# Dividing 648 product columns at 384 instead of 512, and loosening the wait in front of the first routing product

## The chip, the cores and the metric

The kernel runs on one core of one Trainium2 chip. The metric is the device time of one execution in microseconds (us); lower is better. Everything is float32. TensorE multiplies in a rounded format (fp32r), so each operand is kept as a high part and a low part (the value minus its high part), and each product is three matmuls: high by high, high by low, low by high. The high part is made on ScalarE (ACT in the profile), the low part on VectorE (DVE).

## The reference

4096 tokens of width 512 pass through two blocks. Block 0 (a linear layer with per-batch low-rank additions, then a gated feed-forward) has nothing that the change touches. Block 1, in short:

```python
def cond(x, language_ids, W, Wr, A, B):
    base = jnp.einsum('btd,od->bto', x, W)
    logits = x @ Wr.T + 5.0 * one_hot(language_ids)
    gates = top-2 softmax of logits
    h = jnp.einsum('btd,erd->bter', x, A)
    return base + 2.0 * jnp.einsum('bter,bte,eor->bto', h, gates, B)

def ffn(y, W_base, b_base, W_router, A, B):
    gates = top-2 of softmax(y @ W_router.T), renormalised
    h = jnp.einsum('nd,erd->ner', y, A)
    return y @ W_base.T + b_base + 2.0 * (h * gates) @ B

x = x + ffn(cond(x))
```

Both are linear in their input but for the gates, so the kernel multiplies the weights once and runs the tokens through the folded weights.

## The kernel before

Tokens come in eight units of 512, the width in KC = 4 chunks of P = 128, so D = 512. E = 8 experts, and LH = E + 8*16 = 136 is the number of router and low-rank columns of one layer. All engines run their own instruction streams and meet by semaphores. Eight PSUM banks of 128x512 float32 exist: four accumulators (`acc`) and four that are handed out in turn (`ring`).

Block 0 takes about the first 794 us. Then comes **the fold**, `weight_product(i)` for i = 0 to 4: chunk i of the first layer's weights and low-rank factors (128 rows, `m2_hi`/`m2_lo`, the stationary operand) times the second layer's 648 columns (`rhs2_hi`/`rhs2_lo`, the moving operand): the 512 columns of its base weight and the 136 of its router and low-rank factors. Each is a sum over four parts of three matmuls, 12 matmuls to a bank, 24 to a chunk. The 512 columns go to a ring bank called "wide", the 136 to one called "slim".

When "slim" is complete, VectorE adds the identity to the 128 columns i*P of "wide" for i < 4 (the residual path; L1242). ScalarE copies "wide" to `m2_hi` (L921) over the operand just used, then "slim" to `xt_hi` (L924), for i = 4 to `ra2`. VectorE makes the low parts, `m2_lo` (L1244) and `xt_lo` (L1248). These last two free the banks: a ring bank is taken again four uses later, so "wide" of chunk i waits for that of chunk i - 2.

After the fold, TensorE runs `route_x(0)` and `route_x(1)`: for each of 4 token blocks of a unit, 12 matmuls with 272 moving columns, the 136 of the first layer (loaded) and the 136 folded ones. The first of them waits for the low parts of the tokens, for GpSimd's part of `xt_lo`, and for two counts:

```python
e.wait_ge(*ring_freed("wide", KC, 0))
e.wait_ge(*ring_freed("slim", KC - 1, 0))
```

ScalarE splits unit 1 (`split_unit(1)`, L936) between the fold and the copies of the routing banks (L943), VectorE does its half of that (L1229), then the router (`router(0, 0)`, from L1262) whose gated result (L1310) TensorE turns (`turn_h`, L1599). Then `out_base`, `route_h` and `out_close` form the output unit by unit; `out_base` is the first reader of the folded `m2_hi`/`m2_lo`. The helper `mm` at L1438 issues all matmuls but the transposes, so they are told apart by operand names and shapes.

SyncE's queue loads the units: `load_unit(1)` and `load_unit(2)` (L572) are issued when block 0's last matmul is done.

Of the kernel before, what the change touches and what calls it, by code (L numbers as in the profile page):

```python
# [6 lines left out]
ALU = mybir.AluOpType  # L7
ACT = mybir.ActivationFunctionType
AXX = mybir.AxisListType.X

P = 128
# [13 lines left out]
def plain(ap):  # L25
    return ap.bitcast(F32)


def build(nc, x, slots, langs, w0, b0, ab_table, w_gate, w_up, w_down, wb1, rhs2, ra1, b2t, b1, out):
    NT, KC, _, _ = x.shape  # L30
    D = KC * P
# [10 lines left out]
    LH = E + E * R  # L42
# [35 lines left out]
    def work(name, shape, dt):  # L78
        n = W
        for s in shape:  # L80
            n *= s
        h = sb(name, shape, dt, o[0])
        o[0] += (n + 31) // 32 * 32
        assert o[0] <= o[1], name
        return h
# [75 lines left out]
    m2_hi = work("m2_hi", [KC + 1, D], F32R)  # L161
    m2_lo_at = o[0]
    m2_lo = work("m2_lo", [KC + 1, D], F32R)
# [3 lines left out]
    xt_hi = work("xt_hi", [KC, 2 * LH], F32R)  # L167
    xt_lo = work("xt_lo", [KC, 2 * LH], F32R)
    ra2 = work("ra2", [LH], F32)
# [62 lines left out]
    sem = nc.alloc_semaphore  # L232
# [30 lines left out]
    pe_acc, pe_ring = sem("pe_acc"), sem("pe_ring")  # L263
# [16 lines left out]
    c_closed, l_closed = sem("c_closed"), sem("l_closed")  # L280
    act_freed, dve_freed = sem("act_freed"), sem("dve_freed")
    fold_hi_done, fold_lo_done = sem("fold_hi_done"), sem("fold_lo_done")
    m2_eye_done, m2_hi_done, xt_hi_done = sem("m2_eye_done"), sem("m2_hi_done"), sem("xt_hi_done")
    rows_done = sem("rows_done")
    dve_chain = sem("dve_chain")
    diff_done, expo_done, picked_done = sem("diff_done"), sem("expo_done"), sem("picked_done")
# [5 lines left out]
    def nth(t, m=KC - 1):  # L292
        return t * KC + m + 1
# [8 lines left out]
            c_ring += [("h", t + 1, 0, "dve")]  # L302
    l_ring = []
    for i in range(KC + 1):
        l_ring += [("wide", i, 0, "dve"), ("slim", i, 0, "dve" if i < KC else "act")]
    l_ring += [("rx", 0, c, "act") for c in range(TC)] + [("rx", 1, c, "act") for c in range(TC)]
    l_ring += [("th", 0, 0, "dve"), ("rh", 0, 0, "dve"), ("rh", 0, 1, "dve"), ("th", 0, 1, "dve")]
    l_ring += [("th", 1, 0, "dve"), ("rh", 1, 0, "dve"), ("rh", 1, 1, "dve")]
# [17 lines left out]
    def ring_bank(*use):  # L326
        return ring[ring_bank_at[ring_at[use]]]

    def ring_full(*use):
        return ring_at[use] + 1  # L330

    def ring_freed(*use):
        return freed_at[ring_at[use]]
# [76 lines left out]
    def l_slot(t):  # L410
        return t % 3
# [3 lines left out]
    def g_views(n):  # L415
        j, i = divmod(n, 7)
        i = ORDER[i]
        r = j % 2
        src = {1: wg_raw[r][:, 0:2, :], 2: wg_raw[r][:, 2:4, :], 4: wu_raw[r][:, 2:4, :],
               5: gs[r][0], 6: gs[r][1], 7: gs[r][2], 3: gs[r][3]}[i]  # L420
        hi, lo = (wring[n % N_W][:, half:half + 2 * P].rearrange("p (q c) -> p q c", q=2) for half in (0, 2 * P))
        return hi, lo, src[:, :, :]
# [9 lines left out]
        return dt_[n % 4][:, 0:c, 0, :], dt_[n % 4][:, 0:c, 1, :], src  # L432

    S_OF = {5: 1, 6: 2, 7: 3, 3: 4}


    fold_parts = [("wb1", i) for i in range(KC + 1)] + [("rhs2", k) for k in range(KC)]
# [314 lines left out]
    def act_program(e):  # L752
# [36 lines left out]
        def gate_up_hi(n):  # L789
            j, i = divmod(n, 7)  # L790
            i = ORDER[i]
            hi, _, src = g_views(n)
            if i in S_OF:
                e.wait_ge(gs_done, 4 * j + {7: 1, 5: 2, 6: 3, 3: 4}[i])
# [7 lines left out]
        def down_hi(n):  # L802
# [3 lines left out]
            else:  # L806
                g, i = d_steps[n]
                if i in S_OF:
                    e.wait_ge(ds_done, 4 * g + S_OF[i])
                else:  # L810
# [104 lines left out]
            e.activation(hi, first, ACT.Copy).then_inc(fold_hi_done, 1)  # L915

        def weight_product(i):
            e.wait_ge(pe_ring, ring_full("slim", i, 0))
            if i < KC:
                e.wait_ge(m2_eye_done, i + 1)  # L920
            e.activation(m2_hi[:, i, :], ring_bank("wide", i, 0)[:, :], ACT.Copy).then_inc(m2_hi_done, 1)  # L921
            bank = ring_bank("slim", i, 0)
            if i < KC:
                e.activation(xt_hi[:, i, LH:2 * LH], bank[:, 0:LH], ACT.Copy).then_inc(xt_hi_done, 1)  # L924
            else:
                e.activation(ra2[:, :], bank[:, 0:LH], ACT.Copy).then_inc(act_freed, 1)

        def split_unit(t):
            s = l_slot(t)
# [112 lines left out]
        for i in range(KC + 1):  # L1042
            weight_product(i)
# [35 lines left out]
    def dve_program(e):  # L1079
# [157 lines left out]
        def weight_product(i):  # L1237
            if i < KC:

                e.wait_ge(pe_ring, ring_full("slim", i, 0))  # L1240
                own = ring_bank("wide", i, 0)[:, i * P:(i + 1) * P]
                e.tensor_tensor(own, own, ident[:, :], ALU.add).then_inc(m2_eye_done, 1)  # L1242
            e.wait_ge(m2_hi_done, i + 1)
            e.tensor_tensor(m2_lo[:, i, :], ring_bank("wide", i, 0)[:, :], plain(m2_hi[:, i, :]),  # L1244
                            ALU.subtract).then_inc(dve_freed, 1)
            if i < KC:
                e.wait_ge(xt_hi_done, i + 1)
                e.tensor_tensor(xt_lo[:, i, LH:2 * LH], ring_bank("slim", i, 0)[:, 0:LH],  # L1248
                                plain(xt_hi[:, i, LH:2 * LH]), ALU.subtract).then_inc(dve_freed, 1)

        def over(ap):
            return ap[:, :].unsqueeze(2).to_broadcast([P, TC, E])
# [153 lines left out]
        for i in range(KC + 1):  # L1406
            weight_product(i)
# [28 lines left out]
    def pe_program(e):  # L1436
        def mm(out_ap, lhs, rhs, start, stop):
            return e.matmul(out_ap, lhs, rhs, start=start, stop=stop, skip_group_check=True)  # L1438

        def mm3(out_ap, w_hi, w_lo, v_hi, v_lo, start, stop):  # L1440
            mm(out_ap, w_hi, v_hi, start, False)
            mm(out_ap, w_hi, v_lo, False, False)
            return mm(out_ap, w_lo, v_hi, False, stop)

        def take_ring(*use):
            n = ring_at[use]
            first = len(c_ring)
            if n in range(first, first + 4):
                last_of_f = (out11_done, out21_done, out22_done, out12_done)[n - first]
                e.wait_ge(last_of_f, 2 * NS)  # L1450
            elif n >= 4:
                e.wait_ge(*freed_at[n - 4])
            return ring_bank(*use)
# [114 lines left out]
        def weight_product(i):  # L1568
            if i == 0:
                e.wait_ge(fold_lo_done, len(fold_parts))  # L1570
            wide, slim = take_ring("wide", i, 0), take_ring("slim", i, 0)
            for out_ap, cols in ((wide[:, :], slice(0, D)), (slim[:, 0:LH], slice(D, D + LH))):
                for k in range(KC):
                    part = slice(k * P, (k + 1) * P)
                    done = mm3(out_ap, m2_hi[:, i, part], m2_lo[:, i, part],
                               rhs2_hi[:, k, cols], rhs2_lo[:, k, cols], k == 0, k == KC - 1)
                done.then_inc(pe_ring, 1)

        def route_x(t):
            v = l_slot(t)  # L1580
            e.wait_ge(l_lo, nth(t))
            if t == 0:
                e.wait_ge(pool_late, 1)
                e.wait_ge(*ring_freed("wide", KC, 0))
                e.wait_ge(*ring_freed("slim", KC - 1, 0))
            for c in range(TC):
                bank = take_ring("rx", t, c)
                tok = slice(c * P, (c + 1) * P)
                for k in range(KC):
                    done = mm3(bank[:, 0:2 * LH], act_hi[v][:, k, tok], act_lo[v][:, k, tok],  # L1590
                               xt_hi[:, k, :], xt_lo[:, k, :], k == 0, k == KC - 1)
                done.then_inc(pe_ring, 1)
# [9 lines left out]
        def route_h(t):  # L1602
            e.wait_ge(hg1t_done, t + 1)
            if t == 0:
                e.wait_ge(*ring_freed("slim", KC, 0))
            for half in range(2):
                bank = take_ring("rh", t, half)
                for c2 in range(2):
                    c = 2 * half + c2
                    done = mm(bank[:, c2 * LH:(c2 + 1) * LH], hg1t[:, c * P:(c + 1) * P], ra2[:, :], True, True)  # L1610
                done.then_inc(pe_ring, 1)

        def out_base(t, m):
            v = l_slot(t)
            if t == 0:
                e.wait_ge((out11_done, out21_done, out22_done, out12_done)[m], 2 * NS)
            else:
                e.wait_ge(l_closed, nth(t - 1, m))
            if m == 0:
                e.wait_ge(l_lo, nth(t))  # L1620
            cols = slice(m * P, (m + 1) * P)
            for k in range(KC):
                mm3(acc[m][:, :], m2_hi[:, k, cols], m2_lo[:, k, cols],
                    act_hi[v][:, k, :], act_lo[v][:, k, :], k == 0, False)
            if m == 0:
                e.wait_ge(*ring_freed("th", 0, t))
            mm3(acc[m][:, :], m2_hi[:, KC, cols], m2_lo[:, KC, cols],
                hg1_hi[t % 2][:, :], hg1_lo[t % 2][:, :], False, False)
# [44 lines left out]
        for i in range(KC + 1):  # L1673
            weight_product(i)
        route_x(0)
        route_x(1)
        turn_h(0, 0)
        e.wait_ge(pool_late, 2)
# [8 lines left out]
        for m in range(KC):  # L1687
            out_close(0, m)
        route_x(2)
        turn_h(1, 1)  # L1690
        for t in range(1, NT):
# [97 lines left out]
```

## Time and profile before

| | us |
|---|---|
| median of 3 runs | 1025.44 |
| lowest, highest | 1023.64, 1025.75 |
| the profiled execution | 1019.78 |
| its span, first to last instruction | 1018.0 |
| TensorE busy in it | 1001.0 |
| VectorE busy | 550.1 |
| ScalarE busy | 437.9 |
| GpSimd busy | 188.5 |

Times in the rows are from the start of the span, which is 1.78 us shorter than the profiled execution. Matmuls are pipelined and their ends are modelled: the pace of TensorE is read from one start to the next, not from the duration of one matmul.

### The profile page before, as it was taken

The numbers are of one execution on the slowest core, as the hardware profiler recorded it, in microseconds if no ns is written. First come the engines' busy times: TensorE is split into PE (matmuls) and PEld (weight loads), VectorE is DVE, ScalarE is ACT, GpSimd is POOL, SyncE is SP. The second block draws the span as 40 slices with busy tenths as digits, with TensorE's granted clock in tenths as the row PEclk, the third lists the DMA queues.
The fourth block names the chain that finished last, engine by engine and source line by source line (L and its number), as shares of the span: only waits on it lengthen the run. The fifth ranks groups of instructions, "written<-read, shape, count | busy, mean of one in ns | idle before, by whom it ended". The sixth has DMA issues, their size and how long they took to land.

```text
span 1018.0 us, 13873 instructions
## 1 busy us (share of the span) xinstructions
PE 1001.0 (98%) x4835; PEld 841.2 (83%) x4835; DVE 550.1 (54%) x960; ACT 437.9 (43%) x821; POOL 188.5 (19%) x172
## 2 busy tenths in 40 slices
PE   8899998999999999999999999999999999999998
PEld 6888886888888888887888888888878888888886
DVE  3655466877785233586323497233296365555551
ACT  3655456555661333572333373333355133333321
POOL 3332022563400131400113220111350000000000
PEclk9999999999999999999999999999999999999999
DMA  9698667766977776877776777866796302222211
GB/s 320 226 344 296 241 208 274 264 238 235 291 272 232 215 194 194 274 227 258 235 196 193 241 229 253 278 192 196 193 354 222 131 1 84 93 86 91 84 42 62
DMA packets 111404, 210.18 MB, mean 206 GB/s; under 512 B 12260, under 2 KB 12260, under 8 KB 111080
## 3 DMA queue, kind: packets, MB, share of 16 engines
q1 hardware_dynamic: 108800, 200.88, 60.4%
q0 software_dynamic: 2400, 8.41, 2.5%
q8 instruction: 39, 0.64, 0.3%
q14 instruction: 29, 0.24, 0.1%
q10 hardware_dynamic: 136, 0.01, 0.0%
HBM read 154.20 MB, written 55.05 MB: 206 GB/s over the span
## 4 chain that ended last, share of the span: by engine, by line
PE 82%; DVE 11%; DMA 4%; issue 1%; SPq 1%; ACT 1%; POOL 0%; DVEq 0%; ACTq 0%; POOLq 0%
PE bank L1438 81%; DVE op_lo L1160 3%; DVE cop_lo L1146 2%; DMA c<-c_scratch 1%; DMA wring<-wd_scratch 1%; PE bank L1462 1%; PE bank L1599 1%; DMA ab<-in_ab_table,row_i 1%; DVE h_lo L1165 0%; DVE c_t L1142 0%; DMA w_raw<-in_w 0%; DVE c L1151 0%; DVE c L1144 0%; DMA wu_raw<-in_w_up 0%; DVE xa_lo L1089 0%
## 5 line engine op out<-in xcount | busy, mean ns | idle before, releaser
L1438 PE MATMUL bank<-cop_hi,wring 128*128 128x512 f32 x1234 | 381.4, 389 | 2.8 <-ACT bank L853 2.8
L1438 PEld LDWEIGHTS bank<-cop_hi,wring 128*128 128x128 f32 x1234 | 231.7, 188 | 52.2 <-ACT bank L853 3.6
L1438 PE MATMUL bank<-cop_lo,wring 128*128 128x512 f32 x616 | 239.7, 389 | 0.0
L1438 PE MATMUL bank<-op_hi,wring 128*128 128x512 f32 x560 | 174.3, 390 | 1.1 <-DMA wring<-wd_scratch 1.1
L1174 DVE TENSOR_TENSOR v<-bank,p7s 128x512 f32<-128x512 f32 x44 | 30.4, 692 | 195.4 <-PE bank L1438 195.4
L1438 PEld LDWEIGHTS bank<-cop_lo,wring 128*128 128x128 f32 x616 | 115.7, 188 | 23.9
L1438 PEld LDWEIGHTS bank<-op_hi,wring 128*128 128x128 f32 x560 | 105.1, 188 | 24.0 <-DMA wring<-wd_scratch 1.5
L1438 PE MATMUL bank<-op_lo,wring 128*128 128x512 f32 x280 | 108.9, 389 | 0.0
L676 POOL TENSOR_TENSOR h_t<-h,h 128x512 f32<-128x512 f32 x20 | 26.5, 1326 | 383.5 <-DVE h L1193 383.5
L884 ACT ACTIVATE s<-bank 128x512 f32<-128x512 f32 x44 | 26.3, 598 | 122.8 <-PE bank L1438 122.8
L1160 DVE TENSOR_TENSOR op_lo<-h,op_hi 128x512 fp32r<-128x512 f32 x100 | 73.5, 753 | 3.3 <-ACT op_hi L843 3.3
L843 ACT ACTIVATE op_hi<-h 128x512 fp32r<-128x512 f32 x100 | 62.4, 626 | 14.3 <-PE bank L1438 13.6
L1438 PEld LDWEIGHTS bank<-op_lo,wring 128*128 128x128 f32 x280 | 52.6, 188 | 10.8
L853 ACT ACTIVATE bank<-bank 128x512 f32<-128x512 f32 x44 | 25.6, 582 | 77.7 <-PE bank L1438 77.7
L1039 ACT ACTIVATE res<-bank,b 128x512 f32<-128x512 f32 x32 | 22.1, 689 | 76.5 <-PE bank L1438 76.4
L1438 PE MATMUL bank<-xa_hi,w_hi 128*128 128x512 f32 x128 | 51.6, 403 | 1.4 <-DVE w_lo L1093 1.4
L1438 PE MATMUL bank<-act_hi,m_hi 128*128 128x512 f32 x128 | 52.3, 409 | 0.0
L1438 PE MATMUL bank<-xa_lo,w_hi 128*128 128x512 f32 x128 | 50.7, 396 | 0.0
L1438 PE MATMUL bank<-act_hi,m_lo 128*128 128x512 f32 x128 | 50.5, 395 | 0.0
L1438 PE MATMUL bank<-act_lo,m_hi 128*128 128x512 f32 x128 | 50.4, 394 | 0.0
L1438 PE MATMUL bank<-xa_hi,w_lo 128*128 128x512 f32 x128 | 50.4, 393 | 0.0
L1179 DVE TENSOR_TENSOR p7s<-bank,p7s 128x512 f32<-128x512 f32 x44 | 30.4, 690 | 23.4 <-PE bank L1438 23.4
(186 smaller groups left out, 1740.1 us busy)
## 6 DMA issues: line engine op xcount, KB each, us to landing
wring<-wgu_scratch SPq DMA_DIRECT2D x231, 256.0 KB, 2.9
wring<-wd_scratch SPq DMA_DIRECT2D x140, 256.0 KB, 4.6
wgu_scratch<-wring SPq DMA_DIRECT2D x77, 256.0 KB, 3.0
x_raw<-in_x SPq DMA_DIRECT2D x32, 256.0 KB, 5.1
c_scratch<-c_out SPq DMA_DIRECT2D x32, 256.0 KB, 4.2
c<-c_scratch SPq DMA_DIRECT2D x32, 256.0 KB, 4.0
raw<-x_scratch SPq DMA_DIRECT2D x32, 256.0 KB, 3.9
out<-res SPq DMA_DIRECT2D x32, 256.0 KB, 2.0
```

Source lines behind the costliest of these rows:

```text
L676: e.tensor_tensor(h_t3[p][:, :], h22[p][:, :], h12[p][:, :], ALU.subtract).then_inc(t3_done, 1)
L843: e.activation(op_hi[n % N_OP][:, :], op_source[i][p][:, :], ACT.Copy).then_inc(op_hi_done, 1)
L853: e.activation(bank_y[b][:, :], bank_a[b][:, :], ACT.Copy).then_inc(ay_done, 1)
L884: e.activation(s2[j % 2][:, :], bank_z[j % 2][:, :], ACT.Silu).then_inc(silu2_done, 1)
L1039: e.activation(res[m][:, :], acc[m][:, :], ACT.Identity, bias=b1_sb[:, m:m + 1]).then_inc(l_closed, 1)
L1146: e.tensor_tensor(cop_lo[i][:, q, :], cop_source[i][:, :], plain(cop_hi[i][:, q, :]), ALU.subtract).then_inc(cop_lo_done, 1)
L1160: e.tensor_tensor(op_lo[n % N_OP][:, :], op_source[i][p][:, :], plain(op_hi[n % N_OP][:, :]), ALU.subtract).then_inc(op_lo_done, 1)
L1174: e.tensor_tensor(v[b][:, :], bank_z[b][:, :], p7s[b][:, :], ALU.add).then_inc(gc22_done, 1)
L1179: e.tensor_tensor(p7s[b][:, :], bank_y[b][:, :], p7s[b][:, :], ALU.add).then_inc(gc21_done, 1)
L1438: return e.matmul(out_ap, lhs, rhs, start=start, stop=stop, skip_group_check=True)
L1462: done = e.transpose(bank[:, k * P:(k + 1) * P], ab[g][:, k * P:(k + 1) * P], ident[:, :])
L1599: done = e.transpose(bank[:, c * P:(c + 1) * P], flat[:, c, :], ident[:, :])
```

## The change

The 648 columns of a chunk are divided at column 384 instead of 512. The first bank, now called "right", takes columns 384 to 647 (264 of them: the last 128 of the base weight, then the 136), and is multiplied first. The second, "left", takes columns 0 to 383. The copies and subtractions are divided in the same way: one more copy and one more subtraction in each chunk. ScalarE copies the 136 columns when "right" is complete and the rest after "left"; VectorE makes `xt_lo` ahead of the two parts of `m2_lo`. All ring banks of the fold are now freed by VectorE.

The first routing product no longer waits for the two counts quoted above but for the four folded parts of `xt_lo` (a semaphore of their own, `xt_lo_done`). The banks that it takes still have to be free: the four of `route_x(0)` are those of "right" and "left" of chunks 3 and 4. The wait for the last part of `m2_lo` moves to `out_base(0, 0)`.

```diff
-        l_ring += [("wide", i, 0, "dve"), ("slim", i, 0, "dve" if i < KC else "act")]
+        l_ring += [("right", i, 0, "dve"), ("left", i, 0, "dve")]
...
+    CUT = 3 * P
+    def eye_at(i):
+        if i == KC:
+            return None, None
+        return ("left", i * P) if (i + 1) * P <= CUT else ("right", i * P - CUT)
...
         # ScalarE
         def weight_product(i):
-            e.wait_ge(pe_ring, ring_full("slim", i, 0))
-            if i < KC:
+            left, right = ring_bank("left", i, 0), ring_bank("right", i, 0)
+            own = xt_hi[:, i, LH:2 * LH] if i < KC else ra2[:, :]
+            e.wait_ge(pe_ring, ring_full("right", i, 0))
+            e.activation(own, right[:, D - CUT:D - CUT + LH], ACT.Copy).then_inc(xt_hi_done, 1)
+            e.wait_ge(pe_ring, ring_full("left", i, 0))
+            if eye_at(i)[0] == "right":
                 e.wait_ge(m2_eye_done, i + 1)
-            e.activation(m2_hi[:, i, :], ring_bank("wide", i, 0)[:, :], ACT.Copy).then_inc(m2_hi_done, 1)
-            bank = ring_bank("slim", i, 0)
-            if i < KC:
-                e.activation(xt_hi[:, i, LH:2 * LH], bank[:, 0:LH], ACT.Copy).then_inc(xt_hi_done, 1)
-            else:
-                e.activation(ra2[:, :], bank[:, 0:LH], ACT.Copy).then_inc(act_freed, 1)
+            e.activation(m2_hi[:, i, CUT:D], right[:, 0:D - CUT], ACT.Copy).then_inc(m2_hi_done, 1)
+            if eye_at(i)[0] == "left":
+                e.wait_ge(m2_eye_done, i + 1)
+            e.activation(m2_hi[:, i, 0:CUT], left[:, 0:CUT], ACT.Copy).then_inc(m2_hi_done, 1)
...
         # VectorE
         def weight_product(i):
             if i < KC:
-                e.wait_ge(pe_ring, ring_full("slim", i, 0))
-                own = ring_bank("wide", i, 0)[:, i * P:(i + 1) * P]
+                side, at_col = eye_at(i)
+                e.wait_ge(pe_ring, ring_full(side, i, 0))
+                if side == "right":
+                    e.wait_ge(xt_hi_done, i + 1)
+                own = ring_bank(side, i, 0)[:, at_col:at_col + P]
                 e.tensor_tensor(own, own, ident[:, :], ALU.add).then_inc(m2_eye_done, 1)
-            e.wait_ge(m2_hi_done, i + 1)
-            e.tensor_tensor(m2_lo[:, i, :], ring_bank("wide", i, 0)[:, :], plain(m2_hi[:, i, :]),
+            left, right = ring_bank("left", i, 0), ring_bank("right", i, 0)
+            e.wait_ge(m2_hi_done, 2 * i + 1)
+            if i < KC:
+                e.tensor_tensor(xt_lo[:, i, LH:2 * LH], right[:, D - CUT:D - CUT + LH],
+                                plain(xt_hi[:, i, LH:2 * LH]), ALU.subtract).then_inc(xt_lo_done, 1)
+            e.tensor_tensor(m2_lo[:, i, CUT:D], right[:, 0:D - CUT], plain(m2_hi[:, i, CUT:D]),
                             ALU.subtract).then_inc(dve_freed, 1)
-            if i < KC:
-                e.wait_ge(xt_hi_done, i + 1)
-                e.tensor_tensor(xt_lo[:, i, LH:2 * LH], ring_bank("slim", i, 0)[:, 0:LH],
-                                plain(xt_hi[:, i, LH:2 * LH]), ALU.subtract).then_inc(dve_freed, 1)
+            e.wait_ge(m2_hi_done, 2 * i + 2)
+            e.tensor_tensor(m2_lo[:, i, 0:CUT], left[:, 0:CUT], plain(m2_hi[:, i, 0:CUT]),
+                            ALU.subtract).then_inc(dve_freed, 1)
...
         # TensorE
         def weight_product(i):
-            wide, slim = take_ring("wide", i, 0), take_ring("slim", i, 0)
-            for out_ap, cols in ((wide[:, :], slice(0, D)), (slim[:, 0:LH], slice(D, D + LH))):
+            right, left = take_ring("right", i, 0), take_ring("left", i, 0)
+            for out_ap, cols in ((right[:, 0:D - CUT + LH], slice(CUT, D + LH)), (left[:, 0:CUT], slice(0, CUT))):
...
         def route_x(t):
             if t == 0:
                 e.wait_ge(pool_late, 1)
-                e.wait_ge(*ring_freed("wide", KC, 0))
-                e.wait_ge(*ring_freed("slim", KC - 1, 0))
+                e.wait_ge(xt_lo_done, KC)
...
         def route_h(t):
             if t == 0:
-                e.wait_ge(*ring_freed("slim", KC, 0))
+                e.wait_ge(*ring_freed("left", KC, 0))
...
         def out_base(t, m):
+            if t == 0 and m == 0:
+                e.wait_ge(*ring_freed("left", KC, 0))
```

## Rows read from the trace of the kernel before

**Rows 1.** Page, busy time, share of the span and instructions of each engine

```profile
PE 1001.0 (98%) x4835; PEld 841.2 (83%) x4835; DVE 550.1 (54%) x960; ACT 437.9 (43%) x821; POOL 188.5 (19%) x172
```

**Rows 2.** Chain that ended last, around the fold's end: start, us, what

```profile
758.95 56.23 PE bank L1438 x276
...
815.20 0.61 ACT m_hi L921
...
815.83 0.70 DVE m_lo L1244
...
816.74 12.34 PE bank L1438 x96
```

**Rows 3.** TensorE's waits from 790 us on: in total, times, longest

```profile
PE bank L1438 <- DVE m_lo L1244: 1.6, 1, 1.6
PE bank L1599 <- DVE hg L1310: 0.4, 1, 0.4
```

**Rows 4.** Stretches: length, PE, PEld, DVE, ACT, POOL busy, granted clock, DMA share, GB/s

```profile
798.52:802.64 4.12, 4.12 (x26) 3.59 (x26) 1.20 (x3) 0.77 (x2) 0.00 (x0) 1.00 1.02 360
...
810.88:815.17 4.29, 4.29 (x26) 3.61 (x25) 1.20 (x3) 0.77 (x2) 0.00 (x0) 1.00 0.00 0
815.18:816.74 1.56, 0.00 (x1) 0.03 (x1) 0.91 (x2) 1.54 (x4) 0.00 (x0) 1.00 0.00 0
...
864.00:1014.77 150.77, 150.64 (x805) 128.51 (x803) 71.17 (x199) 47.93 (x96) 0.00 (x0) 1.00 0.21 76
```

**Rows 5.** Timeline of TensorE, first and last start of runs of equal matmuls

```profile
799.04 0.39 PE L1438 MATMUL bank<-rhs_hi,m_lo 128*128 128x512 f32 x1
...
801.12 0.40 PE L1438 MATMUL bank<-rhs_hi,m_lo 128*128 128x512 f32 x1
...
801.42 0.27 PE L1438 MATMUL bank<-rhs_lo,m_hi 128*128 128x136 f32 x1
...
802.53 0.28 PE L1438 MATMUL bank<-rhs_hi,m_lo 128*128 128x136 f32 x1
...
817.19 0.29 PE L1438 MATMUL bank<-xt_hi,act_hi 128*128 128x272 f32 x1
...
822.86 0.29 PE L1438 MATMUL bank<-xt_hi,act_hi 128*128 128x272 f32 x1
```

**Rows 6.** Timeline of weight loads beside the 136-column matmuls

```profile
801.47 0.19 PEld L1438 LDWEIGHTS bank<-rhs_hi,m_lo 128*128 128x128 f32 x1
...
802.58 0.19 PEld L1438 LDWEIGHTS bank<-rhs_hi,m_hi 128*128 128x128 f32 x1
```

**Rows 7.** Timeline of ScalarE: one chunk, then the work after the fold

```profile
803.24 0.60 ACT L921 ACTIVATE m_hi<-bank 128x512 fp32r<-128x512 f32 x1 [3.35 <-DVE bank L1242]
803.73 0.28 ACT L924 ACTIVATE xt_hi<-bank 128x136 fp32r<-128x136 f32 x1
...
815.86 2.19 ACT L936 ACTIVATE act_hi<-raw 128x512 fp32r<-128x512 f32 x4
818.52 0.40 ACT L943 ACTIVATE lx<-bank 128x272 f32<-128x272 f32 x1 [0.47 <-PE bank L1438]
```

**Rows 8.** Timeline of VectorE: one chunk, then the work after the fold

```profile
802.85 0.30 DVE L1242 TENSOR_TENSOR bank<-bank,ident 128x128 f32<-128x128 f32 x1 [2.20 <-PE bank L1438]
803.87 0.69 DVE L1244 TENSOR_TENSOR m_lo<-bank,m_hi 128x512 fp32r<-128x512 f32 x1 [0.73 <-ACT m_hi L921]
...
816.53 2.50 DVE L1229 TENSOR_TENSOR act_lo<-raw,act_hi 128x512 fp32r<-128x512 f32 x4
823.49 0.19 DVE L1262 SCALAR_TENSOR_TENSOR logit<-lang_hot,lx 128x32 f32<-128x32 f32 x1 [4.47 <-ACT lx L943]
```

**Rows 9.** Loads of units (issue, landing), and GpSimd's part of xt_lo

```profile
796.59 3.81 SPq L572 DMA_DIRECT2D raw<-x_scratch  x8
...
DMA to landing us min/median/max: 2.7/4.0/4.5
...
L743 POOL TENSOR_TENSOR xt_lo<-ra,xt_hi x1: 1691/1691/1691, 751.3 to 751.3; 128x544 fp32r<-128x544 f32 x1
```

More of the change, by code:

```diff
@@ L282, in build @@
     fold_hi_done, fold_lo_done = sem("fold_hi_done"), sem("fold_lo_done")
-    m2_eye_done, m2_hi_done, xt_hi_done = sem("m2_eye_done"), sem("m2_hi_done"), sem("xt_hi_done")
+    m2_eye_done, m2_hi_done, xt_hi_done, xt_lo_done = (sem(f"{n}_done") for n in ("m2_eye", "m2_hi", "xt_hi", "xt_lo"))
     rows_done = sem("rows_done")
```

## The prediction

> **What bounds the kernel now.** First the page: TensorE is busy for 1001.0 of 1018.0 us, VectorE for 550.1, ScalarE for 437.9 [rows 1]. So time is won only where TensorE waits or where its matmuls need more time than they must. Next the chain that ended last, around the fold: TensorE works without a break to the end of the fold, then the chain goes over ScalarE's copy of the last chunk (0.61 us) and VectorE's subtraction (0.70), and back to TensorE at 816.74 [rows 2]. The list of TensorE's waits from 790 us on has the same place: 1.6 us for `m2_lo`, and besides it one wait of 0.4 us for a gated result [rows 3]. The table of stretches shows the rest: from 864.00 to 1014.77 TensorE is busy for 150.64 of 150.77 us [rows 4]. What makes TensorE earlier in the fold therefore makes the end earlier, unless another engine can't follow. Last, the timeline of TensorE for the pace of each shape, from one start to the next.
>
> **The pace of the matmuls.** Three shapes are in the trace. With 512 columns, nine steps from 799.04 to 801.12: 0.231 us each. With 136 columns, ten steps from 801.42 to 802.53: 0.111. With 272 columns, 45 steps from 817.19 to 822.86: 0.126 [rows 5]. Between 272 and 512 columns a column costs 0.105/240 = 0.00044 us. On that line 136 columns would cost 0.067 us; they cost 0.111, and the loads of the stationary operand beside them start at the same pace, ten steps from 801.47 to 802.58, 0.111 us each [rows 6]. I read this as a floor that the loads set: a 136-column matmul waits for its weights, a 272-column one does not.
>
> The Trainium skill, "TensorE: Matmul & The Clock Gate", section "Back-to-back issue gap", gives columns/2.4 + 2.5 ns for a step. By it a cut anywhere in 648 columns costs the same (12 x 275 = 3.30 us a chunk, an estimate from that page), and this part of the change would give nothing. The trace disagrees where it matters: 0.111 us at 136 columns against the rule's 0.059. The same page's section on LDWEIGHTS has 128/1.2 = 107 ns for a load, and the trace, with 0.111, is near that.
>
> **The change, part by part.**
> *The cut at 384.* Each chunk has 12 matmuls of 512 and 12 of 136 columns, and takes 4.12 us [rows 4]; by the paces above 12 x 0.342 = 4.10. After it, 12 of 264 and 12 of 384. Neither is in the trace. By the line, 264 columns cost 0.126 - 8 x 0.00044 = 0.1225 and 384 cost 0.126 + 112 x 0.00044 = 0.175, together 12 x 0.2976 = 3.57 us. That saves 12 x (0.342 - 0.2976) = 0.53 us a chunk, 2.7 us for five. Bounds from the nearest rows: 264 columns cost no less than 136 (0.111) and no more than 272 (0.126); 384 no less than 272 (0.126) and no more than 512 (0.231). So a chunk takes 2.84 to 4.28 us, between 6.4 us saved and 0.8 lost. I take the line: 264 is nearly the measured 272, and 384 lies midway between two measured sizes.
>
> *The looser wait.* At TensorE's own pace the last chunk, begun at 810.88, would be over at 810.88 + 4.12 = 815.00; the first routing matmul starts at 816.74 [rows 2, 4]. So 1.74 us hang on the high and low parts of the last chunk. What ends last afterwards? Let T be the time when "left" of chunk 4 is complete. `xt_lo` of chunk 3 hangs on "left" of chunk 3, complete 3.57 us before T, then one short ScalarE copy (0.28 at 136 columns [rows 7]) and one short VectorE subtraction (0.30 at 128 [rows 8]) with semaphores between, some 0.9 us in all: ready 2.7 us before T. The banks: those of chunk 3 are free by then too; the third routing block wants "right" of chunk 4 at T + 24 x 0.126 = T + 3.0, free at about T + 0.7; the fourth wants "left" at T + 4.5, free at about T + 1.4. GpSimd's part was made at 751.3, over 40 us before [rows 9]. So nothing stands in the place of the wait, and all 1.74 us go. If the cover of the last chunk's work (12 routing matmuls) were gone, it would cost the 1.4 us.
>
> *More copies and subtractions.* Each chunk has one more of each. From the eye on, a chunk before ran 0.39 us to the ScalarE copy, 0.63 to the subtraction [rows 7, 8]. After: 0.39 to the copy of 384 columns, some 0.5 for it (between 0.40 at 272 and 0.60 at 512), some 0.56 for the subtraction (between 0.30 and 0.69), while `xt_lo` and the right part of `m2_lo` fit behind the eye. That is 1.5 us from the eye, 1.8 from the last matmul's start. "Right" of chunk i + 2 wants its bank 3.57 us after "left" of chunk i is full. All of it lies behind the next chunk's matmuls, with some 1.8 us to spare; cost nothing. If that cover were gone each of three chunks (2, 3, 4) would wait 1.8 us.
>
> *What queues behind.* On ScalarE the split of unit 1 (2.19 us [rows 7]) stands ahead of the copies of the routing banks. TensorE now starts routing at T, but ScalarE is done with the last chunk at T + 0.8 and with the split at T + 3.0, so the first routing bank, full at T + 1.5, is copied 1.5 us late. The next user of that bank comes at T + 6.0, and from the third bank on ScalarE has caught up; nothing. VectorE does its half of the split (2.50 us) by T + 3.9; the router needs it free at 823.49 - 816.74 = 6.75 us after routing starts [rows 2, 8]; nothing. Unit 1 itself is issued from 796.59 over 3.81 us and lands within 4.5 us [rows 9], so by 804.9, while ScalarE now asks for it at about 813: 8 us to spare. The moved wait for the last `m2_lo`, in `out_base(0, 0)` and `route_h(0)`, is met 10 us before TensorE comes there (two routing products at 6.0 us each, less 1.4).
>
> *The wait of 0.4 us* before a transpose [rows 3] ends a chain on VectorE that itself starts from TensorE's first transposes, so it moves with TensorE and stays.
>
> *The granted clock* is 1.00, 2.4 GHz, in the stretch of the stall as in the chunks [rows 4], so to remove the stall neither gains nor loses clock.
>
> **The sum.** 2.7 + 1.74 = 4.4 us, out of the profiled execution's 1019.78: 1015.4, 0.43% less. The median of the runs shown is 5.7 us above that execution, and the stage in question is a fixed run of TensorE work, so I take the same 4.4 us from the median: 1025.44 - 4.4 = 1021.0.
>
> **The rivals.**
> *A: The cut gives nothing*, the stall goes. For it: the cost of a step could be a fixed part and a part per column at all sizes, as the two larger shapes alone would allow; then 648 columns cost the same wherever they are cut. Against it: the 136-column steps are 0.044 us above that line, 60 of them, which is the 2.7 us. It needs a cost at 264 or 384 columns that the neighbours don't show. 1.74 us less: 1023.7. That is the case of the page's rule named above.
> *B: The stall only changes its name.* A bank or `xt_lo` could be late, or the ScalarE copies behind the split. For it: the copy of the first routing bank does come later relative to TensorE. Against: the margins above are 2.3 us and more. 2.7 us less: 1022.7.
> *C: Given back later.* The gated result before the 0.4 us wait, or a load, could be fixed in time rather than moved with TensorE; or other stages differ from run to run by as much. 0 to 2 us less in the end: about 1024.5.
> *D: Slower*, by freeing the banks late. The chain eye, copy, subtraction now has two copies and three subtractions. It decides if it is longer than 3.57 us; then chunks 2, 3 and 4 each wait for the excess. To end 2.05 us above before it has to eat 4.4 us as well: 2.15 us in each of three chunks, a chain of 5.7 us against the 1.8 worked out. With 5.9 us it gives 1028. The single operations are all in the trace at 0.7 us or less, which speaks strongly against it.
>
> **How the numbers follow.** Likeliest case (both parts pay, 4.4 us) 0.76, A 0.05, B 0.06, C 0.09, D 0.04. The measurement tells a change from none at about 0.2%, 2.05 us here. The likeliest and B are beyond it, A (0.17%) and C within: faster 0.82, same 0.14, slower 0.04. Range: the runs before spread over 2.1 us, so the likeliest alone has 1019.5 to 1022.5. Upwards it takes in B and A with a little for the spread, 1023.9. Downwards, where both new shapes are cheaper than the line (264 columns at 0.111 saves 0.7 us more, 384 a little) and the run is a low one, 1018.0.
>
> **What would show it in the profile after.** The fold's chunks each 3.57 us apart instead of 4.12; steps of 0.122 and 0.175 us; the first routing matmul one step behind the last 384-column matmul, no wait for `m2_lo` in the list of waits, and the fold, from its first matmul to the first routing one, 17.9 us long instead of 22.3 (816.74 less 794.4, which is four chunks before 810.88). The first transpose after the routing about 12.1 us after the first routing matmul, as before, and the stretch after 864 as long as before, 4.4 us earlier. Wrong it would be by 384-column steps above 0.19 us, by a new wait inside the fold, or by a wait of over 0.4 us before the later transposes.

## The result and the profile after

| | before | changed |
|---|---|---|
| median of 9 runs | 1023.64 | 1016.12 |
| lowest, highest | 1020.09, 1025.75 | 1014.73, 1019.53 |
| the profiled execution | 1019.78 | 1015.85 |
| its span | 1018.0 | 1014.1 |

The ratio is 0.9938, 95% interval 0.992 to 0.9956: the change makes the kernel faster by 0.62%, 6.3 us (4.5 to 8.2). The direction was forecast, the size was not: 1016.12 us lies below the range of 1018.0 to 1023.9, and the forecast gain of 4.4 us just outside the interval. The ratio puts the gain lower than the two medians, which are 7.5 us apart. The median of before moved too, from the 1025.44 of the three runs shown first to 1023.64 in nine. One execution of the kernel before, in a later batch of 26, took 1646.30 us at a mean granted clock of 0.61 and is left out of all ratios and clock means below.

Now the trace. The page of the changed kernel, busy time of each engine:

```profile
PE 997.6 (98%) x4835; PEld 840.5 (83%) x4835; DVE 556.3 (55%) x965; ACT 439.4 (43%) x826; POOL 192.6 (19%) x172
```

Against [rows 1] TensorE is busy 3.4 us less with as many matmuls; ScalarE and VectorE have five instructions more each. The chain that ended last, where [rows 2] showed it going over ScalarE and VectorE:

```profile
759.48 65.66 PE bank L1455 x372
```

TensorE alone carries it through the fold and both routing products. The waits of TensorE from 790 us on, against [rows 3]:

```profile
PE bank L1615 <- DVE hg L1327: 0.4, 1, 0.4
```

The 1.6 us for `m2_lo` are gone, the 0.4 us are still there. Stretches, columns as in [rows 4]: the second chunk of the fold, the last one, the routing products, and the long stretch behind:

```profile
798.59:802.17 3.58, 3.58 (x26) 3.58 (x25) 1.56 (x5) 1.05 (x3) 0.00 (x0) 1.00 0.91 323
809.31:812.87 3.56, 3.56 (x26) 3.56 (x25) 0.96 (x3) 0.94 (x3) 0.00 (x0) 1.00 0.00 0
812.87:824.97 12.10, 12.10 (x97) 12.10 (x97) 7.27 (x19) 6.82 (x15) 0.00 (x0) 1.00 0.00 0
...
860.00:1010.86 150.86, 150.71 (x806) 128.55 (x803) 71.27 (x199) 48.04 (x96) 0.00 (x0) 1.00 0.21 76
```

A chunk takes 3.56 to 3.58 us instead of 4.12, and TensorE is as full as before in the stretch behind. The timeline of TensorE at the end of the fold:

```profile
811.82 0.34 PE L1455 MATMUL bank<-rhs_hi,m_hi 128*128 128x384 f32 x1
...
812.69 0.34 PE L1455 MATMUL bank<-rhs_hi,m_lo 128*128 128x384 f32 x1
812.87 0.29 PE L1455 MATMUL bank<-xt_hi,act_hi 128*128 128x272 f32 x1
```

Five steps of 384 columns in 0.87 us are 0.174 each, and the first routing matmul comes one such step behind the last. ScalarE and VectorE behind the fold, against [rows 7, 8]:

```profile
813.07 0.28 ACT L934 ACTIVATE m_hi<-bank 128x128 fp32r<-128x128 f32 x1 [1.82 <-PE bank L1455]
813.24 0.49 ACT L937 ACTIVATE m_hi<-bank 128x384 fp32r<-128x384 f32 x1
813.61 2.19 ACT L947 ACTIVATE act_hi<-raw 128x512 fp32r<-128x512 f32 x4
815.70 0.79 ACT L954 ACTIVATE lx<-bank 128x272 f32<-128x272 f32 x2
817.61 0.40 ACT L954 ACTIVATE lx<-bank 128x272 f32<-128x272 f32 x1 [1.11 <-PE bank L1455]
```

```profile
809.82 0.30 DVE L1260 TENSOR_TENSOR xt_lo<-bank,xt_hi 128x136 fp32r<-128x136 f32 x1 [1.73 <-ACT m_hi L934]
...
813.76 0.56 DVE L1265 TENSOR_TENSOR m_lo<-bank,m_hi 128x384 fp32r<-128x384 f32 x1
814.28 2.50 DVE L1240 TENSOR_TENSOR act_lo<-raw,act_hi 128x512 fp32r<-128x512 f32 x4
819.55 0.19 DVE L1279 SCALAR_TENSOR_TENSOR logit<-lang_hot,lx 128x32 f32<-128x32 f32 x1 [2.77 <-ACT lx L954]
```

`xt_lo` is complete at 810.1, 2.7 us before it is wanted; the last subtraction of the fold ends at 814.3, 1.4 us after the routing began. The copy of the first routing bank is late, at 815.70, 2.8 us after the routing began instead of 1.8, and the third is on time again.

So the trace shows the forecast mechanism in its forecast size. From the first matmul of the fold (794.45 before, 795.02 after) to the end of the span it is 223.55 us before and 219.08 after: 4.47 us less, forecast 4.4. Yet the runs differ by 6.3 by the ratio. Where the rest comes from is what the experiments are about.

### The profile page after: what moved, and what is told of

It reads as the page before. It is cut to its first block, busy times and chain, and to the rows that moved or that the text cites. A ratio compares the mean times of both kernels' runs of the same rounds, so it can differ in the third digit from the quotient of the medians.

```text
span 1014.1 us, 13882 instructions
## 1 busy us (share of the span) xinstructions
PE 997.6 (98%) x4835; PEld 840.5 (83%) x4835; DVE 556.3 (55%) x965; ACT 439.4 (43%) x826; POOL 192.6 (19%) x172
## 4 chain that ended last, share of the span: by engine, by line
PE 85%; DVE 7%; DMA 4%; SPq 1%; issue 1%; ACT 1%; POOL 0%; DVEq 0%; ACTq 0%; POOLq 0%
PE bank L1455 84%; DVE op_lo L1171 2%; DVE cop_lo L1157 2%; DMA c<-c_scratch 2%; DMA wring<-wd_scratch 1%; DMA ab<-in_ab_table,row_i 1%; PE bank L1615 1%; PE bank L1479 1%; DMA wu_raw<-in_w_up 0%; DVE xa_lo L1100 0%; DMA w_raw<-in_w 0%; DVE wring L1140 0%; DVE c L1162 0%; DVE c L1155 0%; DVE c_t L1153 0%
```

## The experiments

The reader needs one quantity for each trace: the time from the first matmul of the fold to the end of the span, **F** below. It leaves out block 0, whose length scatters: the fold starts between 793.28 and 798.61 us in the fourteen traces of this study, whatever the kernel. Spans are printed to 0.1 us, so F is good to 0.05. A second quantity comes with every execution, the mean granted clock over its span. In the traces the clock is only at full or at half speed, so (1 - mean) x 1018 us is the time that half clock costs wherever TensorE has work. The times bear this out: over 54 executions of the kernel before, 0.001 less of mean clock goes with 0.9 us more (correlation -0.81).

**One semaphore more.** The changed kernel has a semaphore more than the kernel before, and all behind it are renumbered.

```diff
-    m2_eye_done, m2_hi_done, xt_hi_done = sem("m2_eye_done"), sem("m2_hi_done"), sem("xt_hi_done")
+    m2_eye_done, m2_hi_done, xt_hi_done, xt_lo_done = (sem(f"{n}_done") for n in ("m2_eye", "m2_hi", "xt_hi", "xt_lo"))
```

> The kernel before with one unused semaphore more, at the place where the changed kernel has it, so that all semaphores allocated after it are numbered one higher. Theory 1 (the fold gives 4.4 us, the other 3 of the measured 7.5 are scatter of the stages before the fold): no difference from the kernel before beyond the scatter, -1 to +1 us. Theory 2 (something outside the fold changed for good, with the numbering of semaphores): about 3 us faster than before, in every round.

Measured: 1022.61 us (12 runs) beside 1022.62 of before, ratio 0.9996 (0.9981 to 1.0011). Theory 2 falls. But its trace has F = 225.19 us, 1.6 more than that of before, with the same instructions; the reason comes with the traces below.

**The wait alone.**

```diff
             if t == 0:
                 e.wait_ge(pool_late, 1)
-                e.wait_ge(*ring_freed("wide", KC, 0))
                 e.wait_ge(*ring_freed("slim", KC - 1, 0))
```

> The kernel before with one line taken out: the first routing product no longer waits for the low part of the last fold chunk; the cut stays at 512. Theory 1: 1.74 us faster, the stall of 1.57 us is gone from TensorE's waits, and a chunk of the fold still takes 4.12 us. Rival (the stall only changes its name, since the third routing block still wants the bank of that chunk): a new wait at the third block, and no gain.

Measured: ratio 0.9968 (0.9952 to 0.9985), 3.3 us faster (1.5 to 4.9). In the trace the stall is gone, chunks are as before, and F = 221.83, 1.72 less than the 223.55 of before: the forecast 1.74. The runs gained some 1.5 us more than that, as with the whole change, though the interval reaches down to it. The rival has nothing: no wait at the third routing block.

**The cut alone.**

```diff
             if t == 0:
                 e.wait_ge(pool_late, 1)
-                e.wait_ge(xt_lo_done, KC)
+                e.wait_ge(*ring_freed("left", KC, 0))
```

> The changed kernel with the old wait: the first routing product waits for the last subtraction of the whole fold. Theory 1: 2.7 us faster than the kernel before, chunks of 3.57 us, a stall of about 1.5 us ahead of the routing. Rival (the cut is worth more than the fold shows, as the engines are freer for what stands behind): over 5 us faster.

> The changed kernel with the old wait, one more trace: a stall of 1.5 us. Theory 3: 220.8 us from the fold's first matmul to the end without a fall of the clock (as in the first trace of it), 222.4 with one; the stall is 0.1 us shorter than in the kernel before, so the fall may be seldomer.

Measured: ratio 0.9953 (0.9929 to 0.9976), 4.8 us faster (2.5 to 7.3); the medians differ by 3.6. Both traces have F = 220.82 and 220.84, 2.7 us less than before, the forecast 2.7, a stall of 1.5 us and a full clock behind it.

**The change again.** It ran beside these three.

> The changed kernel as it is, beside the others on the same chip. Theory 1: 4.4 us faster than the kernel before by the medians of many runs (3 to 6), and the sum of the gains of the two half changes. Theory 2: 7.5 us faster, which is the gain of the fold and 3 us that the kernel with the unused semaphore shows as well. The start of the fold within its span should be the same as in the kernel before by theory 1, within what the opening scatters (the waits for gathered rows and the granted clock below 1.00 from 20 to 40 us).

Measured: 1016.90 us, ratio 0.9939 (0.9917 to 0.9961), 6.2 us faster; the medians differ by 5.7. F = 219.08, as in its first trace. Once more the runs gain more than the 4.47 us of the two traces that were compared.

**The kernel before, three more times.** Each is one more trace of the unchanged kernel.

> The kernel before unchanged, for one more trace: theory 3 expects a granted clock below 1.00 in the 8 us after the stall in more than half of such traces (so far in one of two, the kernel with the unused semaphore counted in); theory 1 expects 1.00.

> The kernel before unchanged, one more trace. Theory 3: in most such traces (so far two of three, the kernel with the unused semaphore counted in) the granted clock falls to 0.50 for some 3.4 us after the stall, and the stretch from the first matmul of the fold to the end of the span is about 225.1 us; where it does not fall, 223.5. Theory 1 (no part for the clock): 223.5 whatever the clock.

> As the look before: 225.1 us from the fold's first matmul to the end with the fall, 223.5 without it. With this there are five traces, from which the share of executions with the fall can be told roughly.

F was 225.07, 225.11 and 223.59. Stretches of the first of these: the stall, and the routing behind it.

```profile
818.82:820.42 1.60, 0.03 (x1) 0.03 (x1) 0.90 (x2) 1.53 (x4) 0.00 (x0) 1.00 0.00 0
820.42:822.00 1.58, 1.58 (x11) 1.58 (x12) 1.58 (x3) 1.32 (x3) 0.00 (x0) 0.87 0.00 0
822.00:824.00 2.00, 2.00 (x11) 2.00 (x10) 0.71 (x2) 0.40 (x1) 0.00 (x0) 0.50 0.00 0
824.00:826.00 2.00, 2.00 (x14) 2.00 (x14) 0.00 (x0) 0.40 (x1) 0.00 (x0) 0.75 0.00 0
826.00:834.11 8.11, 8.11 (x66) 8.11 (x65) 3.94 (x13) 3.40 (x7) 0.00 (x0) 1.00 0.00 0
```

The third number from the right is the granted clock: 1.00 in the stall itself, and 0.50, the level of 1.2 GHz, soon after TensorE has taken up work again at 820.42. The timeline shows it matmul by matmul:

```profile
821.25 0.28 PE L1438 MATMUL bank<-xt_hi,act_hi 128*128 128x272 f32 x1
821.37 0.29 PE L1438 MATMUL bank<-xt_lo,act_hi 128*128 128x272 f32 x1
...
822.10 0.43 PE L1438 MATMUL bank<-xt_hi,act_lo 128*128 128x272 f32 x1
822.33 0.43 PE L1438 MATMUL bank<-xt_hi,act_hi 128*128 128x272 f32 x1
...
825.03 0.29 PE L1438 MATMUL bank<-xt_hi,act_hi 128*128 128x272 f32 x1
825.16 0.29 PE L1438 MATMUL bank<-xt_lo,act_hi 128*128 128x272 f32 x1
```

Steps of 0.13 us become 0.23, the first of them at 821.65, and are 0.13 again from 825.03 on. The third of these traces is without the fall, same stretches:

```profile
819.33:820.90 1.57, 0.00 (x1) 0.03 (x1) 0.91 (x2) 1.54 (x4) 0.00 (x0) 1.00 0.00 0
820.90:833.07 12.17, 12.17 (x96) 12.17 (x97) 6.24 (x17) 5.50 (x12) 0.00 (x0) 1.00 0.00 0
```

The two routing products take 12.17 us here and 13.69 there (820.42 to 834.11). With the kernel with one semaphore more and the first trace, that makes three falls in five traces of a stall of 1.6 us, each at 1.5 us.

**The stall filled with work.** If the idle time brings the fall about, then useless matmuls in its place must prevent it.

```diff
             if t == 0:
+                e.wait_ge(*ring_freed("slim", KC - 1, 0))
+                for _ in range(7):
+                    mm(acc[3][:, :], m2_hi[:, 0, 0:P], act_hi[0][:, 0, :], True, True)
                 e.wait_ge(pool_late, 1)
                 e.wait_ge(*ring_freed("wide", KC, 0))
```

> The kernel before with seven more 512-column matmuls into a free accumulator bank between the fold and the first routing product (their result is not used). They fill the stall with 7 x 0.231 = 1.6 us of work, so routing starts when it started before. Theory 3 (the stall costs its 1.74 us, and in most executions, after it, a stretch of about 3.4 us at half the TensorE clock, another 1.7 us, as the trace of the kernel with the unused semaphore shows): 1.0 to 1.7 us faster than the kernel before though it has more work, mean granted clock 0.9965 instead of 0.995. Theory 1 (the gain is the idle time alone, the rest is scatter of the opening): no difference, or 0.1 us slower.

Stretches of its trace, the filler and the routing:

```profile
818.80:820.39 1.59, 1.59 (x9) 1.17 (x8) 0.84 (x2) 1.47 (x4) 0.00 (x0) 1.00 0.00 0
820.39:832.51 12.12, 12.12 (x97) 12.12 (x97) 6.29 (x17) 5.56 (x12) 0.00 (x0) 1.00 0.00 0
```

The clock stays at 1.00 and F = 223.44, that of a trace without the fall. As two of five traces of the stall itself have no fall either, this one proves little alone; the mean clock of its 12 executions, 0.9968 against 0.9953 for the 29 of the kernel before beside them, says more. In time it is inconclusive: ratio 0.9988 (0.9966 to 1.001), 1.2 us faster, within which both theories lie.

**A longer stall.** In the place of the old wait comes one for unit 1's low part, for its first quarter or for all of it.

```diff
                 e.wait_ge(*ring_freed("wide", KC, 0))
+                e.wait_ge(l_lo, nth(1, 0))       # stall_plus; nth(1, 3) in stall_long
```

> The kernel before with the first routing product waiting also for the first quarter of unit 1's low part, so that the stall is about 2.2 us instead of 1.6. Theory 3: 0.5 us slower for the longer stall and as much again as the clock falls in more executions: 0.5 to 1.2 us. Theory 1: 0.5 us slower, mean granted clock as before, 0.995.

> The same with the whole low part of unit 1: a stall of about 4.1 us. Theory 3: 2.4 us slower for the stall itself, and in the profile half clock after it for 3 us or more, so 2.4 to 4.5 us slower in all, mean granted clock 0.993 to 0.994. Theory 1: 2.4 us slower and clock 0.995.

Stretches of both traces, the stall and the routing; the first two rows are of the shorter one:

```profile
816.43:818.84 2.41, 0.01 (x1) 0.04 (x1) 1.75 (x3) 2.38 (x6) 0.00 (x0) 1.00 0.00 0
818.84:832.52 13.68, 13.68 (x96) 13.68 (x97) 5.38 (x16) 4.65 (x10) 0.00 (x0) 0.88 0.00 0
```

```profile
813.96:818.22 4.26, 0.04 (x2) 0.03 (x1) 3.19 (x5) 2.84 (x6) 0.00 (x0) 0.87 0.00 0
818.22:832.94 14.72, 14.72 (x96) 14.72 (x97) 3.96 (x13) 4.19 (x9) 0.00 (x0) 0.81 0.00 0
```

Both fall. The shorter costs 1.5 us in the routing as before, the longer 2.55. In the runs: ratio 1.0019 (1.0 to 1.0039), 1.9 us slower, where 0.5 to 1.2 were expected by theory 3, and 1.0046 (1.0024 to 1.0067), 4.7 us slower, where the longer idle time alone (4.26 us instead of 1.57) would be 2.7 and theory 3 expected 2.4 to 4.5. The mean clocks are 0.9949 and 0.9923: the first tells the theories apart no better than the time does, the second lies below even theory 3's 0.993 to 0.994.

**Another cut.**

```diff
-    CUT = 3 * P
+    CUT = 2 * P
```

> The changed kernel with the columns divided at 256 instead of 384: 392 columns to the right bank, 256 to the left. If above the floor a column costs the same everywhere (12 x (0.1785 + 0.119) us), a chunk takes 3.57 us as with the cut at 384. Rival (the gain of the cut at 384 is something of that division, such as the eye added in parallel): another chunk time. No stall ahead of the routing in either case, 219.1 us from the fold's first matmul to the end.

The timeline of one chunk:

```profile
797.70 0.34 PE L1455 MATMUL bank<-rhs_hi,m_hi 128*128 128x392 f32 x1
...
799.84 0.28 PE L1455 MATMUL bank<-rhs_hi,m_hi 128*128 128x256 f32 x1
...
801.25 0.34 PE L1455 MATMUL bank<-rhs_hi,m_hi 128*128 128x392 f32 x1
```

3.55 us, steps of 0.178 and 0.118; F = 219.00. The cut at 384 has nothing of its own: it is enough that neither part is on the floor. The one run took 1018.45 us, in which the start of the fold at 797.70 (795.02 in the trace of the changed kernel) has its share.

All traces together:

| kernel | stall | clock falls after it | F |
|---|---|---|---|
| before, five traces (one with a semaphore more) | 1.6 | no, yes, yes, yes, no | 223.55, 225.19, 225.07, 225.11, 223.59 |
| stall filled | none | no | 223.44 |
| longer stall | 2.4 | yes | 225.99 |
| long stall | 4.2 | yes | 228.82 |
| wait alone | none | no | 221.83 |
| cut alone, two traces | 1.5 | no, no | 220.82, 220.84 |
| the change, two traces | none | no, no | 219.08, 219.08 |
| cut at 256 | none | no | 219.00 |

The mean clocks of the executions line up with it: 0.9951 (54 executions) and 0.9948 (12) with the stall of 1.6 us; 0.9967 (12, the wait alone), 0.9968 (12, filled) and 0.9966 (16, the change) without a stall; 0.9961 (8) with the cut alone.

These means hold more than this one stall. Earlier, in block 0, around 165 to 175 us, TensorE waits 1.8 to 3.0 us for a bank in every one of the fourteen traces, and in eight of them the clock falls too, near the end of that wait or up to 1.2 us behind it. The stretch around it without a fall (the first trace of before) and with one (the first further trace):

```profile
166.00:180.00 14.00, 11.84 (x52) 9.44 (x51) 8.34 (x15) 7.34 (x18) 6.05 (x8) 1.00 1.01 367
166.00:180.00 14.00, 11.88 (x45) 9.20 (x44) 6.75 (x13) 7.63 (x18) 5.93 (x8) 0.88 0.98 346
```

The eight start the fold at 797.47 to 798.61 us, the other six at 793.28 to 796.21, so a good part of block 0's scatter goes with this fall. The length of the wait does not decide it (a fall with 1.86 us, none with 3.01). From 190 us to the stall of the fold no trace loses clock.

## Why the prediction was right and wrong

*The cut at 384: right.* Forecast steps of 0.1225 and 0.175 us, a chunk of 3.57; measured 0.123, 0.174 to 0.175 and 3.56 to 3.58. The reading of the 136-column steps as standing on a floor holds: with no part below 256 columns a chunk costs 3.55 to 3.58 us at either cut. The prediction had "three shapes" in the trace; there were more, and they would have backed it: 256 columns at 0.120 us a step, on the line (0.119), and four transposes of 128 columns from 828.91 at 0.109, nearly the pace of 136.

That the loads set the floor rested on weaker ground: every matmul has a load of its own, so equal paces prove nothing. The timeline of the kernel before, where the 512 columns end and the 136 begin, says more:

```profile
801.12 0.19 PEld L1438 LDWEIGHTS bank<-rhs_hi,m_hi 128*128 128x128 f32 x1
801.35 0.22 PE L1438 MATMUL bank<-rhs_hi,m_hi 128*128 128x136 f32 x1
801.36 0.19 PEld L1438 LDWEIGHTS bank<-rhs_lo,m_hi 128*128 128x128 f32 x1
801.42 0.27 PE L1438 MATMUL bank<-rhs_lo,m_hi 128*128 128x136 f32 x1
801.47 0.19 PEld L1438 LDWEIGHTS bank<-rhs_hi,m_lo 128*128 128x128 f32 x1
801.53 0.28 PE L1438 MATMUL bank<-rhs_hi,m_lo 128*128 128x136 f32 x1
```

Among the 512-column matmuls a load starts together with the matmul ahead of its own (both at 801.12 [rows 5]), and so does the load at 801.36; the first 136-column step takes 0.07 us, as the line has it. The next load starts at 801.47, 0.11 behind the load before it and 0.05 behind the matmul at 801.42, and its matmul follows at 801.53. That fits a floor from the loads; no run changed the loads to test it.

The rule of the Trainium skill that was weighed there ("TensorE: Matmul & The Clock Gate", "Back-to-back issue gap", columns/2.4 + 2.5 ns) has no such floor, and by it the cut would have given nothing; the runs side with the rows. The section itself calls this the gap of an isolated matmul, which counts too little at small sizes because the weight load is not in it. It is also 10 to 13 ns short at 264 and 384 columns (112.5 and 162.5 ns against 123 and 175).

*The looser wait: right as far as it goes.* 1.72 us of idle time gone in the kernel with the wait alone, forecast 1.74; no bank, no copy and no load came in its place. Margins were as worked out (`xt_lo` 2.7 us early).

*More copies and subtractions, what queues behind, the 0.4 us wait: right.* Nothing in the fold waits; the first routing bank is copied late and nobody waits for it; the stretch behind is as long as before. The rivals A to D all fall: A by the chunk time, B by the list of waits, C and D by F.

*The granted clock: wrong.* "To remove the stall neither gains nor loses clock" was read off one trace in which the clock was 1.00 in the stall and the routing took its 12.17 us. That trace was one of the two in five without the fall. In the three others the same stall is followed by a stretch at 0.50 that costs 1.5 us, so the stall cost 1.74 us in some executions and 3.3 in others. That idle time brings it about is shown by the traces: no fall in the five without a stall (the one filled with useless work among them), a fall in both with a longer one, and none anywhere else from 190 us to the last half microsecond of the span. The traces are few, though, and the share of executions with a fall is known only roughly. By the traces it is 3 in 5, which makes the mean gain 4.47 + 0.6 x 1.55 = 5.4 us (five traces leave the share open from about 0.15 to 0.95, and the gain from 4.7 to 5.9). By the mean granted clock it is a little more: 0.9951 over 54 executions of the kernel before, 0.9966 over 16 of the changed one, unrounded 0.0014 x 1018 = 1.4 us, together 5.9. The falls in block 0 are in these means as well, so this is uncertain by about 0.9 us.

The same executions give a check of the whole. Their mean times are 1022.46 and 1016.81 us, 5.65 apart. With (1 - mean clock) x 1018 taken from each time they are 1017.52 and 1013.31, 4.2 apart, with 0.6 either way (95%). So what is left when the clock is taken out agrees with the forecast 4.4, and the other 1.4 go with the clock.

*From the span to the median: wrong in the reference and too narrow.* The forecast took 4.4 us from 1025.44. Nine runs have 1023.64, further batches 1022.6 and 1022.1: 1.8 to 3.3 us of the miss were in the number subtracted from. By the medians of the 54 and 16 executions, 1022.28 and 1016.20, the miss of 4.9 us (1021.0 against 1016.12) is 3.2 us of reference and 1.7 of gain, so the reference, and not the clock, is the larger part of it. And the range gave the changed kernel's scatter 1.5 us on each side, where the start of the fold alone moves over 5.3 us between traces. The two batches put the gain at 6.3 and 6.2 us (4.5 to 8.2 and 4.0 to 8.5); 5.4 to 5.9 lies well within both. Nothing is left that would need another cause.

*Open:* whether a slightly shorter stall (1.5 us in the kernel with the cut alone) falls more seldom. Both of its traces were without a fall, and its runs gained 3.6 us by the medians and 4.8 by the ratio, more than its 2.7 us of TensorE work, which would fit a rarer fall but also the scatter. The waits in block 0, where the clock fell with 1.86 us and not with 3.01, speak against a simple rule by length.

## What to carry to other kernels

Divide the columns of a product so that no part is so small that its steps stand on the floor (0.111 us at 136 columns): here 512 + 136 cost 4.12 us and 384 + 264, or 392 + 256, 3.56, with the same matmuls and the same columns. When a wait of TensorE is priced, look in several executions at the granted clock *behind* it, not only in it: one trace can show the cheap case. And take the reference from more runs than three when a stage ahead of the change scatters by more than the change is worth. Where each execution has its mean clock on record, take the lost clock out of the times first: here that left 4.2 us of a raw 5.65, which is the change itself.

## What the runs showed of the hardware that was not expected

An idle stretch of TensorE of 1.57 to 1.66 us, after hundreds of microseconds of nearly full work at 2.4 GHz, was followed in three of five traces by some 3.4 us at 1.2 GHz, which began only 0.8 to 1.2 us after the work had resumed. An idle stretch of 4.2 us, in which the clock fell before its end, lost 2.55 us more in the routing behind it. With seven 512-column matmuls of useless work in the stall the clock stayed up in the one trace, and at 0.9968 in the mean of 12 executions. And a matmul of 136 columns takes 0.111 us from start to start, where the line through larger ones has 0.067, with 128-column weight loads at the same pace beside it; the first such matmul behind the 512-column ones takes 0.07.
